# A fused sequence model block on one core: the injections of every second round of scan blocks 6 to 11 made beside attention, and the first experts' loads set apart

## The chip, the core and the metric

The kernel runs on one core of one Trainium2 chip. Five engines work side by side, each through its own list of instructions: PE (TensorE, matmuls), DVE (VectorE), ACT (ScalarE), POOL (GpSimd) and SP (SyncE), which here only issues DMAs. They are held together by semaphores: an instruction can wait until a counter has reached a number, and all that stands behind it in the list of its engine then waits too. The metric is device time in microseconds, from start to end of one execution; smaller is better. Between two versions of this kernel a difference of about 0.2%, or 2.6 us, can just be told from none.

## What is computed

Two layers over a sequence of 2048 tokens with 128 channels. The second layer carries nearly all of the time, and the change is in it alone: a selective scan in both directions, an attention with 16 heads whose sums go through a mixture of eight experts, and the sum of both.

```python
def step(h, ins):                       # 256 channels x 16 states, 2048 steps, forward and backward
    dt_t, u_t, B_t, C_t = ins
    h = exp(dt_t[..., None] * A) * h + (dt_t * u_t)[..., None] * B_t[:, None, :]
    y_t = einsum('bdn,bn->bd', h, C_t)
...
y = (y + u * Dp) * silu(z)
out_scan = einsum('bld,ed->ble', y, Wout)
...
o = softmax(q @ k.T / sqrt(D)) @ v      # 16 heads of 8 channels
x = x + (o @ wo + bo)
idx = argmax(layernorm(x) @ gate_w + gate_b)
moe = y_of_expert[idx]                  # relu(h @ w1[e] + b1[e]) @ w2[e] + b2[e]
return x + moe
```

(The inputs of the attention and of the scan are both normed from the same x; `out_scan` of both directions and the attention's result are added.)

## The kernel before

**Three stages** follow each other. `layer0_stage` computes the first layer. `front_stage` computes the attention and, ahead of it and beside it, the inputs of the scan, which go to DRAM: dt, dt times u (`dtu_d`), u, z, and the rows of B and C (`bc_d`). `tail_stage`, from about 878 us on, runs the scan, and beside it the experts.

**The scan** is cut into 8 chunks of 512 steps (4 forward, 4 backward), each chunk into 2 blocks of 128 channels: 16 blocks, numbered 0 to 15. A block is done in 4 rounds (q = 0 to 3, four of the 16 states each), a round in 4 tiles (j = 0 to 3, 32 channels each). A tile is 128 partitions x 512 steps. Rounds are numbered r = 0 to 63 and tiles k = 4r + j; block i has the rounds 4i to 4i + 3. Block 0 is done during attention; the loop of the tail runs over rounds 4 to 63. A tile takes four steps:

- ACT makes the decay exp(dt A) in one of four PSUM banks (line 1608), and later copies the last column of the state to `last` (line 1620);
- POOL makes the **injection** dtu times B, for two tiles (0 and 1, or 2 and 3) in one instruction of 128x1024 into `inject`, four tiles deep (line 1536);
- DVE runs the **scan** over decay and injection (line 1811), in place in PSUM, or into one of four buffers `hp` when POOL is to weigh the tile;
- the **weighing** with C goes to `hc`, which has two buffers, one for each parity of the round. `on_pool(k)` says which tiles are weighed by POOL (line 1521, 128x512 each); the others are DVE's (line 1737), tiles 1 and 2 as one instruction of 128x1024 where both are its own. In a round of blocks 5 to 12 POOL weighs tile 0, and tile 3 too where r % 3 is 1.

PE then adds the 4 tiles of a round into `y_bank` (line 1943, `sums(r)`), and in the first round of each block DVE multiplies the finished block before it with z after its tile 3 (line 1748, `gate`). A weighing in round r waits for `summed` of round r - 2, and a gate for the sums of all rounds of its block.

**Order on POOL.** The loop over tiles makes the injection of tiles j, j + 1 at an even tile, and then weighs the tile that lies three back, if it is POOL's: `weigh(k - NI + 1)` with NI = 4. An injection waits until the scan of the tile whose buffer it takes is done.

**Blocks made ahead.** POOL is nearly idle in attention. For the blocks in `AHEAD` (1 to 4 and 13 to 15) `products` (line 755) makes the injections of tiles 2 and 3 of all four rounds there, one block in each of the attention steps s = 2 to 8, four instructions of 128x1024. SP loads their inputs one step earlier (`load_for_products`) and stores the results to `ahead_d`. In the tail SP brings them back, one round of 512 KB at a time, into three buffers `ahead` (`load_ahead`, line 1412), and waits for that until the scans of the round that used the buffer are done. An ahead round has no injection of tiles 2 and 3 on POOL; in exchange POOL weighs tiles 0 and 3 there, and in odd rounds tile 2.

**Order on SP in the tail.** A loop over rounds: ahead loads, in every fourth round the dt and dtu of the next block (`load_steps`, line 410, eight DMAs), in some rounds the four arrays of an expert for slot s (`load_expert`, line 1432 and on, in round 19 + 4n + m for slot 3n + m), in round 20 the gathered rows for all 23 slots in four DMAs (`load_rows`, line 1424), and u and z of the next block (line 428). PE takes the first rows in `turn_rows(0)` of round 20 (line 1886), before `sums(21)`.

**Block 0's inputs.** In attention steps 10 to 14 SP loads B and C for block 0 and the first rounds (`load_bc`, line 436, one set a step). POOL makes its injections in steps 13 to 15 (`early_inject`, line 769, pairs 0 and 1, then 2 to 4, then 5 to 7; pair p needs the set p // 2). In each step they stand ahead of `split_max` (line 742), which attention needs.

## Time and profile before

| | us |
|---|---|
| median of 3 runs | 1314.99 |
| lowest and highest | 1313.97, 1315.51 |
| the profiled execution | 1312.72 |
| its span, first to last instruction | 1311.0 |

The span is 1.7 us shorter than the profiled execution's own time; this lies around it. A profile shows for each engine when it was busy, and for an idle stretch what ended it. In the tail two or more engines are busy more than nine tenths of the time, so the busy shares alone don't say what bounds it; the order of single instructions, and which of them waits for which, has to be read.

### The profile page before, as it was taken

The page shows a single profiled execution, that of the slowest core. Times are in us where ns is not written, and L with a number is a line of the kernel's source. Part 1 is how long each engine was busy: PE and PEld are TensorE (multiplying, and loading weights), DVE is VectorE, ACT ScalarE, POOL GpSimd, SP SyncE. Part 2 cuts the span into 40 slices and gives each one's busy share as a digit, 9 for nine tenths or more (in the row PEclk, how much of TensorE's full clock was granted, in tenths as well). Part 3 has the DMA queues.
Part 4 walks back from the last instruction along what each step waited for, and adds up shares of the span by engine and source line. Part 5 has one row for each costly group of instructions (what it writes and reads, how often), then busy time and mean ns, then how long its engine had stood idle before and what let it go on. Part 6 is the DMA issues. An engine that isn't in the chain of part 4 may idle for free. (4 is left out here: it accounts for less than half of the span.)

```text
span 1311.0 us, 18381 instructions
## 1 busy us (share of the span) xinstructions
PE 1034.7 (79%) x6017; PEld 337.0 (26%) x6017; DVE 1175.0 (90%) x1728; ACT 891.9 (68%) x1352; POOL 545.3 (42%) x395
## 2 busy tenths in 40 slices
PE   2789996888888888888888888884755987978764
PEld 1443331111111111111111111131411444444311
DVE  7892667999999999999999999848899899999997
ACT  6354558777777777777778787876545667777642
POOL 5020112502332023300000302226779899999896
PEclk9989996999999999999999999995656587888766
DMA  3034332314303464220000010016648966675452
GB/s 102 0 109 166 143 130 82 124 49 114 113 19 124 141 160 133 61 80 30 17 17 21 13 34 18 1 58 164 156 129 213 215 173 155 167 174 155 117 163 63
DMA packets 92385, 134.50 MB, mean 103 GB/s; under 512 B 15059, under 2 KB 45578, under 8 KB 92290
## 3 DMA queue, kind: packets, MB, share of 16 engines
q1 hardware_dynamic: 91266, 131.23, 36.0%
q0 software_dynamic: 1024, 2.10, 0.6%
q8 instruction: 48, 0.79, 0.3%
q14 instruction: 47, 0.39, 0.1%
HBM read 92.75 MB, written 40.24 MB: 101 GB/s over the span
## 5 line engine op out<-in xcount | busy, mean ns | idle before, releaser
L923 DVE TENSOR_REDUCE at_mpart<-psum 128x1 f32<-128x512 f32 x1024 | 637.8, 684 | 42.2 <-PE psum L1104 39.0
L895 ACT ACTIVATE at_probs<-psum 128x1024 f32<-128x1024 f32 x512 | 495.4, 1022 | 141.1 <-PE psum L1134 140.3
L1104 PE MATMUL psum<-at_ks,at_qs 56*128 56x512 bf16 x1024 | 202.3, 392 | 101.1 <-DVE at_mpart L923 100.4
L1147 PE MATMUL psum<-at_probs,at_vg 128*32 128x512 f32 x2048 | 273.6, 606 | 0.7 <-ACT at_probs L895 0.6
L1536 POOL TENSOR_TENSOR t_inject<-shared 128x1024 f32<-128x1024 f32 x92 | 215.6, 2355 | 29.4 <-POOLq L60 19.3
L742 POOL CAST at_m<-at_mneg 128x16 bf16<-128x16 f32 x16 | 4.0, 252 | 481.6 <-DVE at_mneg L928 476.0
L1608 ACT ACTIVATE psum<-shared,aneg 128x512 f32<-128x512 f32 x240 | 164.0, 691 | 48.7 <-DVE t_hc L1737 37.9
L1134 PE MATMUL psum<-at_qs,at_ks 59*128 59x512 bf16 x1024 | 156.6, 378 | 7.4 <-ACT at_probs L895 6.2
L1104 PEld LDWEIGHTS psum<-at_ks,at_qs 56*128 56x128 bf16 x1024 | 49.3, 93 | 423.5 <-DVE at_mpart L923 408.1
L1943 PE MATMUL psum<-t_hc,stack 128*32 128x512 f32 x480 | 95.5, 880 | 74.6 <-POOL t_hc L1521 48.5
L1521 POOL TENSOR_TENSOR t_hc<-t_hp,shared 128x512 f32<-128x512 f32 x100 | 126.0, 1271 | 32.6 <-DVE t_hp L1811 30.2
L1811 DVE TENSOR_TENSOR_SCAN psum<-psum,last,t_inject 128x512 f32<-128x512 f32 x88 | 109.0, 1274 | 5.6 <-ACT psum L1608 4.3
L1737 DVE TENSOR_TENSOR t_hc<-psum,shared 128x1024 f32<-128x1024 f32 (+1 forms) x90 | 86.8, 964 | 0.0
L1859 PE MATMUL psum<-t_bc_rows,t_sel 32*128 32x512 f32 x108 | 81.9, 896 | 0.0
L1620 ACT ACTIVATE last<-psum 128x1 f32<-128x1 f32 x99 | 16.5, 167 | 92.8 <-DVE t_hc L1737 92.4
L1811 DVE TENSOR_TENSOR_SCAN t_hp<-psum,last,t_inject 128x512 f32<-128x512 f32 x56 | 71.3, 1272 | 6.1 <-ACT psum L1608 3.5
L755 POOL TENSOR_TENSOR shared<-shared 128x1024 f32<-128x1024 f32 x28 | 65.2, 2360 | 0.0
L1134 PEld LDWEIGHTS psum<-at_qs,at_ks 59*128 59x128 bf16 x1024 | 50.1, 96 | 57.1 <-ACT at_probs L895 27.1
L728 POOL TENSOR_TENSOR shared<-shared 128x1024 f32<-128x1024 f32 x8 | 22.3, 2806 | 98.0 <-DVE shared L975 98.0
L1076 PE MATMUL psum<-mp_xm,mp_taps 128*128 128x512 f32 x128 | 61.6, 632 | 0.0
L1147 PEld LDWEIGHTS psum<-at_probs,at_vg 128*32 128x32 f32 x2048 | 40.3, 108 | 61.4 <-issue 59.5
L1943 PEld LDWEIGHTS psum<-t_hc,stack 128*32 128x32 f32 x480 | 12.8, 129 | 120.1 <-POOL t_hc L1521 69.8
(262 smaller groups left out, 1143.9 us busy)
## 6 DMA issues: line engine op xcount, KB each, us to landing
shared<-mp_dt_d SPq DMA_DIRECT2D x64, 256.0 KB, 5.8
mp_ahead_d<-shared SPq DMA_DIRECT2D x7, 2048.0 KB, 7.9
t_ahead<-mp_ahead_d SPq DMA_DIRECT2D x28, 512.0 KB
t_w<-in_w SPq DMA_DIRECT2D x46, 256.0 KB
shared<-mp_bc_d SPq DMA_DIRECT2D x152, 64.0 KB, 3.0
shared<-mp_dtu_d SPq DMA_DIRECT2D x36, 256.0 KB, 9.3
shared<-mp_dtu_d SPq DMA_DIRECT2D x56, 128.0 KB, 4.3
...
```

Of the source, the lines that this page charges most:

```text
L895: act.activation(probs[:, u_ % 2, p, :], s_pair[p], ACT.Exp, scale=float(HD) ** -0.5).then_inc(probs_ready, 1)
L923: dve.reduce_max(mpart[:, s % 2, 2 * jp + b, i, kc:kc + 1], ring[x % 3], AX.X).then_inc(ring_free, 1)
L1104: pe.matmul(ring[z_ % 3], qs[half(b, DQ), buf, of_pair(jp, c * CH + i * P, P)], ks[half(b, DQ), buf, of_pair(jp, kc * CH, CH)], start=True ...
L1134: mm = pe.matmul(s_banks[p][b], ks[half(b, DM), g % 2, of_pair(p, kt * P, P)], qs[half(b, DM), g % 2, of_pair(p, c * CH, CH)], start=True, ...
L1147: mm = pe.matmul(o_bank[VW * j:VW * (j + 1), :], vg[:, g % 2, kt, j, :], probs[:, u_ % 2, j // 2, CH * (j % 2):CH * (j % 2 + 1)], start=(k ...
L1521: pool.tensor_tensor(hc[:, r % 2, j, :], hp[:, by_pool[k] % NHP, :], cs[:, (NQ * (i // NB) + q) % NBC, :], ALU.mult).then_inc(pool_weighed, 1)
L1536: pool.tensor_tensor(inject[:, x % NI:x % NI + 2, :], dus[:, i % 2, j:j + 2, :], bs[:, m % NBC, :].unsqueeze(1).to_broadcast([P, 2, CH]), ...
L1608: act.activation(decay[k % ND], dts[:, i % 2, j, :], ACT.Exp, scale=S.aneg[:, n // NCH, m:m + 1])\
L1737: dve.tensor_tensor(hc[:, r % 2, j:j + n, :], decays[:, j:j + n, :], cs[:, m % NBC, :].unsqueeze(1).to_broadcast([P, n, CH]), ALU.mult).th ...
L1811: dve.tensor_tensor_scan(h, decay[k % ND], added, last[:, k % PC:k % PC + 1] if n % NCH else 0.0, ALU.mult, ALU.add).then_inc(scanned, 1)
L1859: pe.matmul(out, sel[:, NQ * o + q, :], bc_rows[:, n % 2, :], start=True, stop=True).then_inc(side_full, 1)
L1943: mm = pe.matmul(y_bank[GC * j:GC * (j + 1), :], S.stack[:, :], hc[:, r % 2, j, :], start=False, stop=(q == NQ - 1), tile_position=(0, GC ...
```

## The change

`AHEAD` becomes a list of groups of 8 pairs of tiles at most. The seven blocks of before stay. Three groups are new, of two blocks each (6 and 7, 8 and 9, 10 and 11): of these only rounds q = 1 and 3 are made ahead, so 12 rounds, all with an odd number. `AHEAD_AT` gives the place of a round in `ahead_d`. The products of the new groups are made in attention steps 9 to 11, and the loads of B and C for block 0 are moved from steps 10 to 14 into steps 12 to 14 (sets 0 and 1, then 2 and 3, then 4).

```diff
-AHEAD = 1, 2, 3, 4, 13, 14, 15
+AHEAD = [((i,), range(NQ)) for i in (1, 2, 3, 4, 13, 14, 15)] + [((2 * n, 2 * n + 1), (1, 3)) for n in (3, 4, 5)]
+AHEAD_AT = {(i, q): (g, m * len(qs) + x) for g, (blocks, qs) in enumerate(AHEAD)
+            for m, i in enumerate(blocks) for x, q in enumerate(qs)}
...
-                if s == 10:
+                if s == 12:
                     sp.wait_ge(a_st, 16 * len(AHEAD))
-                if 10 <= s < 10 + Inputs.NBC:
-                    first.load_bc(S, sp, s - 10, first_in[s - 4])
+                if 12 <= s < 15:
+                    for m in ((0, 1), (2, 3), (4,))[s - 12]:
+                        first.load_bc(S, sp, m, first_in[m + 6])
...
+            def products(g):
+                pool.wait_ge(a_in, 16 * SP4 * sum(len(blocks) + len(qs) for blocks, qs in AHEAD[:g + 1]))
+                if g:
+                    pool.wait_ge(a_st, 16 * g)
+                blocks, qs = AHEAD[g]
+                for m in range(len(blocks)):
+                    for x in range(len(qs)):
+                        pool.tensor_tensor(first.products[:, m * len(qs) + x, :, :], first.some_dus[:, m, :, :],
+                                           first.some_bs[:, x, :].unsqueeze(1).to_broadcast([P, 2, CH]), ALU.mult).then_inc(a_made, 1)
...
         def is_ahead(k):
 
-            return k // PB in AHEAD and k % NJ >= 2
+            return (k // PB, k // NJ % NQ) in AHEAD_AT and k % NJ >= 2
 
         def on_pool(k):
             r, j = divmod(k, NJ)
             if SCATTER <= r < SCATTER + MOVE or GATHER <= r < GATHER + MOVE:
-                return r // NQ in AHEAD and (j == 0 or j == 3 and r % 2 == 1)
-            if r // NQ in AHEAD:
+                return is_ahead(NJ * r + 2) and (j == 0 or j == 3 and r % 2 == 1)
+            if is_ahead(NJ * r + 2):
                 return j in (0, 3) or j == 2 and (r < SCATTER or r % 2 == 1)
-            return j == 0 or j == 3 and r % 3 == 1
+            return j == 0 or j == 3 and r % 3 == 1 and not is_ahead(NJ * r + 6)
...
-                if (s := slot_at(r, -2)) is not None:
+                if 0 <= r - FIRST_SLOT + 6 < W:
+                    load_expert(r - FIRST_SLOT + 6)
+                if (s := slot_at(r, -2)) is not None and s >= W:
                     load_expert(s)
...
-                if r == SCATTER + MOVE:
-                    for n in range(NX):
-                        load_rows(n)
+                if r >= SCATTER + MOVE and (r - SCATTER - MOVE) % 6 == 0 and (r - SCATTER - MOVE) // 6 < NX:
+                    load_rows((r - SCATTER - MOVE) // 6)
```

So in the odd rounds of blocks 6 to 11 POOL makes one injection in place of two and weighs tiles 0, 2 and 3; in their even rounds it makes two injections and weighs tile 0 alone. The experts of slots 0 to 3 are loaded in rounds 15 to 18 instead of 19, 20, 21 and 23, and the four parts of the gathered rows in rounds 20, 26, 32 and 38. The other edits size the buffers for a group of two blocks (in `Inputs`, `load_steps`, `load_for_products`) and look up the place of a round in `load_ahead`.

**POOL, rounds 24 to 27 (block 6).** `t_inject` is an injection of two tiles, `t_hc<-t_hp` a weighing. Before:

```order
L1536 TENSOR_TENSOR t_inject<-shared 128x1024 x2
L1521 TENSOR_TENSOR t_hc<-t_hp,shared 128x512
L1536 TENSOR_TENSOR t_inject<-shared 128x1024 x2
L1521 TENSOR_TENSOR t_hc<-t_hp,shared 128x512
L1536 TENSOR_TENSOR t_inject<-shared 128x1024 x2
L1521 TENSOR_TENSOR t_hc<-t_hp,shared 128x512 x2
```

And after, rounds 24 to 26 and the first injection of round 27:

```order
L1545 TENSOR_TENSOR t_inject<-shared 128x1024
L1545 TENSOR_TENSOR t_inject<-shared 128x1024
L1530 TENSOR_TENSOR t_hc<-t_hp,shared 128x512
L1545 TENSOR_TENSOR t_inject<-shared 128x1024
L1530 TENSOR_TENSOR t_hc<-t_hp,shared 128x512
L1545 TENSOR_TENSOR t_inject<-shared 128x1024
L1530 TENSOR_TENSOR t_hc<-t_hp,shared 128x512
L1545 TENSOR_TENSOR t_inject<-shared 128x1024
L1530 TENSOR_TENSOR t_hc<-t_hp,shared 128x512 x2
L1545 TENSOR_TENSOR t_inject<-shared 128x1024
```

In row 4 stands the one injection of round 25, and in row 5, right behind it, the weighing of tile 0 of that same round. Before, the injection of tiles 2 and 3 stood between the two.

**DVE, the end of round 27 to round 29 (blocks 6 and 7).** `psum` and `t_hp` are scans, by where they write; `t_gated` is the gate. After:

```order
L1820 SCALAR_TENSOR_TENSOR t_hp<-psum,last,t_ahead 128x512
L1820 SCALAR_TENSOR_TENSOR t_hp<-psum,last,t_inject 128x512
L1820 SCALAR_TENSOR_TENSOR psum<-psum,last,t_inject 128x512
L1677 TENSOR_TENSOR res<-res,psum 128x512
L1820 SCALAR_TENSOR_TENSOR psum<-psum,last,t_inject 128x512 x2
L1746 TENSOR_TENSOR t_hc<-psum,shared 128x1024
L1757 TENSOR_TENSOR t_gated<-shared,psum 128x512
L1820 SCALAR_TENSOR_TENSOR t_hp<-psum,last,t_inject 128x512
L1746 TENSOR_TENSOR t_hc<-psum,shared 128x512
L1820 SCALAR_TENSOR_TENSOR psum<-psum,last,t_inject 128x512
L1820 SCALAR_TENSOR_TENSOR t_hp<-psum,last,t_ahead 128x512
L1746 TENSOR_TENSOR t_hc<-psum,shared 128x512
```

Before, tile 0 of round 28 to the gate:

```order
L1811 SCALAR_TENSOR_TENSOR t_hp<-psum,last,t_inject 128x512
L1737 TENSOR_TENSOR t_hc<-psum,shared 128x512
L1811 SCALAR_TENSOR_TENSOR psum<-psum,last,t_inject 128x512
L1668 TENSOR_TENSOR res<-res,psum 128x512
L1811 SCALAR_TENSOR_TENSOR psum<-psum,last,t_inject 128x512
L1811 SCALAR_TENSOR_TENSOR t_hp<-psum,last,t_inject 128x512
L1737 TENSOR_TENSOR t_hc<-psum,shared 128x1024
L1748 TENSOR_TENSOR t_gated<-shared,psum 128x512
```

The even round keeps its weighings of 128x1024 and, behind tile 0 of the next round, of 128x512; the odd round has one of 128x512 left.

**SP, round 20.** Before, from `load_steps` on:

```order
L410 DMA shared<-mp_dt_d 32x4x512 x4
L410 DMA shared<-mp_dtu_d 32x4x512 x4
L1432 TENSOR_LOAD t_eid
L1432 ISA x2
L1433 ISA
L1433 DMA t_w1<-in_w1 128x512
L1434 ISA
L1434 DMA t_b1<-in_b1 128x4
L1435 DMA t_w2<-in_w2 128x4x128
L1437 ISA
L1437 DMA t_b2<-in_b2 1x128
L1424 DMA t_x<-t_rows 128x6x128 x3
```

After, down to the loads for the next block:

```order
L1420 DMA t_ahead<-mp_ahead_d 128x1024 x2
L412 DMA shared<-mp_dt_d 32x4x512 x4
L412 DMA shared<-mp_dtu_d 32x4x512 x4
L1432 DMA t_x<-t_rows 128x6x128
L433 DMA shared<-mp_u_d 128x512
L433 DMA shared<-mp_z_d 128x512
```

The expert has gone from ahead of the rows, and one part of the rows is loaded there instead of four.

## Rows read from the trace of the kernel before

**Rows 1.** The page: the span, and the busy time of each engine.

```profile
span 1311.0 us, 18381 instructions
PE 1034.7 (79%) x6017; PEld 337.0 (26%) x6017; DVE 1175.0 (90%) x1728; ACT 891.9 (68%) x1352; POOL 545.3 (42%) x395
```

**Rows 2.** Windows of the tail: length, busy us per engine, clock, DMA share.

```profile
1029.70:1043.00 13.30, 13.30 (x40) 7.29 (x39) 9.27 (x10) 8.91 (x23) 10.93 (x7) 0.50 0.86 197
1045.30:1202.10 156.80, 129.89 (x686) 70.26 (x685) 154.07 (x146) 109.43 (x294) 150.98 (x81) 0.83 0.71 167
```

**Rows 3.** DVE in order of time: start, duration, what; round 27 into 28.

```profile
1066.29 0.67 DVE L1737 TENSOR_TENSOR t_hc<-psum,shared 128x512 f32<-128x512 f32 x1
1066.87 1.28 DVE L1811 TENSOR_TENSOR_SCAN psum<-psum,last,t_inject 128x512 f32<-128x512 f32 x1
1068.06 0.67 DVE L1668 TENSOR_TENSOR res<-res,psum 128x512 f32<-128x512 f32 x1
...
1071.01 1.20 DVE L1737 TENSOR_TENSOR t_hc<-psum,shared 128x1024 f32<-128x1024 f32 x1
1072.13 0.68 DVE L1748 TENSOR_TENSOR t_gated<-shared,psum 128x512 f32<-128x512 f32 x1
1072.72 1.28 DVE L1811 TENSOR_TENSOR_SCAN t_hp<-psum,last,t_inject 128x512 f32<-128x512 f32 x1
```

**Rows 4.** POOL in order of time, around round 33.

```profile
1095.31 4.68 POOL L1536 TENSOR_TENSOR t_inject<-shared 128x1024 f32<-128x1024 f32 x2
1099.94 1.27 POOL L1521 TENSOR_TENSOR t_hc<-t_hp,shared 128x512 f32<-128x512 f32 x1
1101.18 4.67 POOL L1536 TENSOR_TENSOR t_inject<-shared 128x1024 f32<-128x1024 f32 x2
```

**Rows 5.** DVE: the scans of tile 0 in rounds 25 and 47.

```profile
1045.88 1.27 DVE L1811 TENSOR_TENSOR_SCAN t_hp<-psum,last,t_inject 128x512 f32<-128x512 f32 x1
...
1189.27 1.27 DVE L1811 TENSOR_TENSOR_SCAN t_hp<-psum,last,t_inject 128x512 f32<-128x512 f32 x1
```

**Rows 6.** POOL at round 52, the first ahead round behind block 12.

```profile
1218.89 2.35 POOL L1536 TENSOR_TENSOR t_inject<-shared 128x1024 f32<-128x1024 f32 x1
1223.26 1.27 POOL L1521 TENSOR_TENSOR t_hc<-t_hp,shared 128x512 f32<-128x512 f32 x1 [2.02 <-DVE t_hp L1811]
```

**Rows 7.** DVE: the scan of tile 0 in round 52.

```profile
1221.91 1.27 DVE L1811 TENSOR_TENSOR_SCAN t_hp<-psum,last,t_inject 128x512 f32<-128x512 f32 x1
```

**Rows 8.** The chain that ended last, in order of time, near 1018 us.

```profile
1018.00 7.66 DMA t_x<-t_rows
```

**Rows 9.** SP in order of time, round 20.

```profile
1008.67 4.46 SPq L410 DMA_DIRECT2D shared<-mp_dtu_d  x4
```

**Rows 10.** PE in order of time, rounds 20 to 23.

```profile
1025.80 0.45 PE L1886 MATMUL psum<-ident,t_x 128*128 128x128 f32 x1 [2.57 <-DMA t_x<-t_rows]
1026.17 1.93 PE L1943 MATMUL psum<-t_hc,stack 128*32 128x512 f32 x8
...
1033.96 1.94 PE L1943 MATMUL psum<-t_hc,stack 128*32 128x512 f32 x8
...
1043.89 1.21 PE L1943 MATMUL psum<-t_hc,stack 128*32 128x512 f32 x8
```

**Rows 11.** DVE in round 21 into 22.

```profile
1023.21 0.66 DVE L1737 TENSOR_TENSOR t_hc<-psum,shared 128x512 f32<-128x512 f32 x1
```

**Rows 12.** POOL in attention: two groups of products, an early injection, the next split_max.

```profile
500.09 9.31 POOL L755 TENSOR_TENSOR shared<-shared 128x1024 f32<-128x1024 f32 x4
541.41 9.31 POOL L755 TENSOR_TENSOR shared<-shared 128x1024 f32<-128x1024 f32 x4
...
752.32 2.35 POOL L769 TENSOR_TENSOR mp_w_in<-shared 128x1024 f32<-128x1024 f32 x1
787.88 0.20 POOL L742 CAST at_m<-at_mneg 128x16 bf16<-128x16 f32 x1 [33.21 <-DVE at_mneg L928]
```

**Rows 13.** SP in attention: loads of B and C in steps 11 to 13.

```profile
673.25 3.66 SPq L436 DMA_DIRECT2D shared<-mp_bc_d  x8
714.57 4.65 SPq L436 DMA_DIRECT2D shared<-mp_bc_d  x8
...
755.80 4.49 SPq L436 DMA_DIRECT2D shared<-mp_bc_d  x8
```

42 lines of the change are left out of this document (19 added, 23 removed).

## The prediction

> **What bounds the kernel now.** I read the page first [rows 1]: a span of 1311.0 us, DVE busy for 90% of it, POOL for 42%. The change moves work out of rounds 24 to 47 of the tail, so the window over these rounds comes next [rows 2]: 156.8 us long, DVE busy 154.07, POOL 150.98. Both are full there, and neither number says what a change on both brings. For that I read single instructions. On DVE a scan takes 1.19 us from start to start, a weighing of 128x512 0.58, one of 128x1024 1.12, and a gate or an addition to `res` 0.59 [rows 3]. On POOL two injections take 4.63, so 2.31 each, and a weighing 1.24 [rows 4].
>
> A pair of rounds, one even (E) and one odd (O), is the unit of the changed pattern. Before, DVE has in it 8 scans (9.52), two weighings of 1024 (2.24), on average 1.33 of 512 (0.77; 16 of the 24 rounds have one), half a gate and a quarter of an addition (0.44): 12.97 us. POOL has 4 injections (9.24) and 2.67 weighings (3.31): 12.55 us. The measured pair takes (1189.27 - 1045.88) / 11 = 13.04 us [rows 5]. So DVE bounds these rounds, with POOL half a microsecond behind it, and every other engine has room.
>
> **The change, rounds 24 to 47, by busy time.** POOL loses 12 injections (12 x 2.31 = 27.7) and gains 16 weighings (from 32 to 48: 16 x 1.24 = 19.8): 7.9 us less. DVE: in the 12 odd rounds the weighing of 1024 becomes one of 512 (12 x 0.54 = 6.5), 8 of them lose the one of tile 3 (8 x 0.58 = 4.6), and 4 even rounds get one back (2.3): 8.8 us less. Per pair DVE would need 12.97 - 0.73 = 12.24, POOL 3 x 2.31 + 4 x 1.24 = 11.89. If nothing else counted, the rounds would be 8.8 us faster.
>
> **The same, by order.** What counts is what each waits for. In the changed list of POOL the weighing of tile 0 of an odd round stands directly behind the injection that this tile needs. DVE can't scan O0 before the injection has ended, and POOL can't go on before the scan has: POOL stands for one whole scan in each pair. The trace has one such place, at round 52: injection at 1218.89, weighing of the same tile at 1223.26 with 2.02 us idle before it, released by DVE [rows 6]; the scan between them starts at 1221.91, and from its start to POOL's is 1.35 us [rows 7]. From one O0 to the next the loop is: weighing O0, injection E01, weighing O2, injection E23, weighings O3 and E0, injection O01, scan O0, which is 4 x 1.24 + 2 x 2.31 + 2.35 (the last injection, to its end) + 1.35 = 13.28 us. No buffer shortens it, since the list of POOL holds all of it. DVE fits in: with the end of scan O0 as 0, E2 can start at 7.2 (its injection ends then), E3 at 8.4, the weighing at 9.6, a gate at 10.7 to 11.3, and O0 comes at 12.0; DVE is idle about 1 us a pair. The pair thus takes 13.28 instead of 13.04. Eleven pairs cost 11 x 0.24 = 2.6 us; in the four that lie in rounds 32 to 39 a scan without a state from before is some 0.05 shorter, which I leave out. The start of round 24 and the end of round 47 I take as equal. Term: **+2.6 us** instead of -8.8.
>
> **PE at the gates.** POOL's weighing of O3 ends at 8.4 on this scale, 2.3 us ahead of the gate; on DVE it stood 4.7 us ahead of it (three scans and a weighing of 1024). And `sums` of the odd round stands behind PE's side work of the even one. At the lower clock (0.50, so 1.2 GHz) an even round with B and C to spread and all three expert steps keeps PE from 1033.96 to 1043.89, 9.9 us [rows 10]. It starts at 0.6, so `sums(O)` would start at 10.5 and end at 12.4, where the gate is due at 10.7; O0 then comes at 13.0, 1.0 us late. This can happen at the gates of rounds 32, 40 and 48, whose even rounds have the spreading. At the higher clock it can't. The window has a mean clock of 0.83 [rows 2], so I take one of three: **+1.0 us**, bounds 0 and 3.0.
>
> **Block 5, rounds 20 to 23.** The chain that ended last goes through the load of the rows, from 1018.00 for 7.66 us [rows 8]. PE sits idle for 2.57 us, from 1023.23, until they land, and does `sums(21)` at 1026.17 [rows 10]. Then it is busy without a gap at the lower clock to 1043.89, and DVE, which waits for ACT and by it for PE, is busy 9.27 of the 13.3 us from 1029.70 [rows 2]: 4.0 us idle. In the change SP issues the first part of the rows right behind `load_steps`, whose last DMA ends at 1008.67 + 4.46 = 1013.13 [rows 9], 4.9 us earlier; with the same 7.66 us it lands at 1020.8, before PE asks for it. `sums(21)` then waits for the weighing of tile 3 alone, which ends at 1023.87 [rows 11], and starts 2.3 us earlier. As PE is the bound up to 1043.89, DVE gets these back one for one: **-2.3 us**. The bounds are 0 (the rows land no earlier) and -4.0 (all the idle time of DVE).
>
> A rule bears on that lower bound. In the trace the clock is 0.50 while PE is busy without a gap from 1029.70 to 1043.00, and at 1043.89 the same sums take 1.21 us instead of 1.94 [rows 2, 10]. The Trainium skill, TensorE: Matmul & The Clock Gate, Part 1, says that the throttled clock is the resting state and that activity lifts it. By that rule a PE without the gap at 1023 would be fast sooner, and the term would be up to -4.0 in place of -2.3. The trace has no run without the gap, so the sum stays with -2.3.
>
> **What is hidden.** *Products in attention*: 12 more instructions on POOL, three times 9.31 us. Two steps with products start 541.41 - 500.09 = 41.32 apart [rows 12], two without 714.57 - 673.25 = 41.32 [rows 13]. Cost 0, bound 0.1 a step; the cover is POOL's idle time in a step of 41 us. *B and C of block 0 two steps later*: pair 4 of the early injections ran at 752.32, and its set is now issued from 755.80 on [rows 12, 13]. POOL waits there some 10 us, with `split_max` queued behind; but that one starts at 787.88 only after 33 us of idle time for DVE's maxima. Cost 0. *Experts 0 to 3 in rounds 15 to 18*: SP issues about 2 to 4 us more in each, ahead of loads that are due two rounds (13 us) later. Nothing waits for them in the trace of before; cost 0, with the bound of one late transfer as PE saw it, 2.6 us [rows 10]. *The 12 ahead loads*: 6.3 MB more in a window that moved 167 GB/s with DMA busy 0.71 [rows 2]; 24% more bytes make that 0.88. They are issued four rounds ahead. A gain could come only from the thinner traffic in rounds 19 to 23; it is in the -4.0.
>
> **Sum.** +2.6 + 1.0 - 2.3 = +1.3 us on the profiled execution's 1312.72 (span 1311.0 and 1.7 around it), so 1314.0. The median of the runs is 2.3 above that execution; on it the forecast is 1314.99 + 1.3 = **1316.3 us**.
>
> **Rivals.** *DVE stays the bound and its savings count.* It speaks for it that DVE is busier than POOL in the window and both lose 8 to 9 us; against it, the loop above, which the list of POOL fixes. If the loop took less than 12.24: -8.8 - 2.3 = -11.1, 1303.9 us. *PE decides.* If PE is at 1.2 GHz before all three gates, and the rows bring nothing because the rest of the traffic is as dense (0.86 in block 5 [rows 2]): +2.6 + 3.0 = +5.6, 1320.6 us. It decides from the point where `sums` of an odd round starts later than 9.5 us behind scan O0. This is the case that ends on the slower side. *The spacing of the loads does nothing*, the rest as forecast: +3.6, 1318.6. *The clock rises sooner in block 5 and no gate is late*: +2.6 - 4.0 = -1.4, 1313.6.
>
> **How the numbers follow.** A difference under 0.2% (2.6 us) can't be told from none. The forecast with its own range of 1313.6 to 1318.6 has a chance of 0.60; DVE's savings in whole or large part 0.16; PE at the gates, late transfers or both, above 1318.6, 0.19; something between 1306 and 1313 0.05. Faster than 1312.4 is then 0.19. Slower than 1317.6 is the 0.19 and a part of the forecast's own range (0.13): 0.32. The same: 0.49. The range from 1311 to 1322 leaves out the first rival and little else.
>
> **What would show it.** In the profile after: POOL idle some 1.3 us before the weighing that follows the single injection of each odd round, released by a scan into `t_hp`; tile 0 of rounds 25 and 47 some 146 us apart instead of 143.4; DVE idle about 12 us in these rounds, ended by POOL's injection; no wait of PE for `t_x` in round 20, and the sums of round 23 some 2.3 us earlier against round 20. The forecast is wrong if that distance comes out near 135 us (the loop is no loop), or over 149 (PE or DMA decides), or if attention's steps are longer than 41.3 us.

## The result, and the profile after

| | before | after |
|---|---|---|
| median (20 runs each) | 1315.26 us | 1318.03 us |
| lowest and highest | 1310.09, 1318.50 | 1315.55, 1321.86 |
| span of the profiled execution | 1311.0 us | 1315.6 us |

The ratio is 1.0022, with a 95% interval of 1.0015 to 1.0030: the changed kernel is slower by 2.9 us. The interval leaves out 1, but it reaches to both sides of the 0.2% that can just be told from none. The forecast was 1316.3, with a range of 1311 to 1322. By the prediction's own classes, 1318.03 lies just inside "slower than 1317.6", to which it had given 0.32, and not in "the same", with 0.49.

The page of the changed kernel, its span and its busy times, answers to [rows 1]:

```profile
span 1315.6 us, 18475 instructions
PE 1039.8 (79%) x6017; PEld 338.2 (26%) x6017; DVE 1167.0 (89%) x1724; ACT 892.9 (68%) x1352; POOL 566.9 (43%) x411
```

DVE has 8.0 us less to do than before and the span is 4.6 us longer, so the saved work became waiting. To see where, I cut the span at three gates, which DVE does at the end of rounds 20, 24 and 48 (start, duration, instruction):

```profile
1015.99 0.67 DVE L1757 TENSOR_TENSOR t_gated<-shared,psum 128x512 f32<-128x512 f32 x1
...
1043.88 0.68 DVE L1757 TENSOR_TENSOR t_gated<-shared,psum 128x512 f32<-128x512 f32 x1
...
1206.64 0.67 DVE L1757 TENSOR_TENSOR t_gated<-shared,psum 128x512 f32<-128x512 f32 x1
```

The same three gates stand at 1014.32, 1045.29 and 1202.12 in the kernel before. So:

| stretch | before | after | difference |
|---|---|---|---|
| start to gate of round 20 | 1014.3 | 1016.0 | +1.7 |
| block 5, to gate of round 24 | 31.0 | 27.9 | -3.1 |
| blocks 6 to 11, to gate of round 48 | 156.8 | 162.8 | +5.9 |
| to the end | 108.9 | 109.0 | +0.1 |

**Blocks 6 to 11.** The windows of the changed kernel over the end of block 5 and over these six blocks (length; busy us of PE, PEld, DVE, ACT and POOL; granted clock, DMA share, GB/s) answer to [rows 2]:

```profile
1029.45:1043.00 13.55, 13.55 (x52) 7.10 (x50) 12.27 (x12) 10.16 (x30) 12.79 (x7) 0.65 0.44 93
1043.88:1206.64 162.76, 134.10 (x686) 71.65 (x684) 146.75 (x142) 109.61 (x293) 142.54 (x84) 0.80 0.81 206
```

In the second row DVE is idle for 16.0 us and POOL for 20.2; before it was under 3 us and about 6 [rows 2]. By releaser the profile puts most of DVE's idle time down to ACT's decays (10.6 us) or to nothing that it shows (4.9). The times of the single scans say otherwise: 10.6 us of it lie before scans that start 0.1 us behind the end of a POOL injection, with the decay ready 1.2 us or more before. The forecast had about 12 us, ended by the injection. Another 3.2 us belong to one slow pair of rounds, described below. The reason stands in POOL's list, here around round 33 (start, duration, instruction, and in brackets the idle time before it and what ended it):

```profile
1095.41 2.35 POOL L1545 TENSOR_TENSOR t_inject<-shared 128x1024 f32<-128x1024 f32 x1
1099.19 1.27 POOL L1530 TENSOR_TENSOR t_hc<-t_hp,shared 128x512 f32<-128x512 f32 x1 [1.43 <-DVE t_hp L1820]
1100.43 2.37 POOL L1545 TENSOR_TENSOR t_inject<-shared 128x1024 f32<-128x1024 f32 x1
1102.76 1.26 POOL L1530 TENSOR_TENSOR t_hc<-t_hp,shared 128x512 f32<-128x512 f32 x1
1103.99 2.34 POOL L1545 TENSOR_TENSOR t_inject<-shared 128x1024 f32<-128x1024 f32 x1
1106.29 2.48 POOL L1530 TENSOR_TENSOR t_hc<-t_hp,shared 128x512 f32<-128x512 f32 x2
1108.74 2.35 POOL L1545 TENSOR_TENSOR t_inject<-shared 128x1024 f32<-128x1024 f32 x1
```

The order is the one of the prediction's loop. After the single injection of the odd round POOL stands still for 1.43 us until DVE has scanned tile 0; that is the one wait of POOL in the loop (1.39 to 1.45 us in ten of the twelve odd rounds), and from one such injection to the next it takes 1108.74 - 1095.41 = 13.33 us. Before, POOL went straight from the injections into the weighing [rows 4].

From tile 0 of round 25 (1044.47) to tile 0 of round 47 (1193.57) it is 149.10 us; before it was 143.39 [rows 5]. Ten of the eleven pairs take 13.28 to 13.40 us, 13.33 on average. One, from round 39 to round 41, takes 15.76. There DVE waits three times, for ACT, whose decays end right before these scans start:

```profile
1146.79 1.29 DVE L1820 TENSOR_TENSOR_SCAN psum<-psum,last,t_inject 128x512 f32<-128x512 f32 x1 [1.97 <-ACT psum L1617]
1148.50 1.29 DVE L1820 TENSOR_TENSOR_SCAN psum<-psum,last,t_inject 128x512 f32<-128x512 f32 x1 [0.41 <-ACT psum L1617]
1150.61 1.29 DVE L1820 TENSOR_TENSOR_SCAN psum<-psum,last,t_inject 128x512 f32<-128x512 f32 x1 [0.82 <-ACT psum L1617]
```

ACT in turn waits for PE's spread of B and C (first row), and PE is at its lower level: behind a wait of 3.36 us for POOL it becomes slower, and a spread takes 3.78 us instead of 1.98, or 1.2 in place of 2.4 GHz (the other two rows):

```profile
1145.58 0.60 ACT L1582 ACTIVATE shared<-psum 128x512 f32<-128x512 f32 x1 [1.87 <-PE psum L1868]
```

```profile
1134.18 1.57 PE L1952 MATMUL psum<-t_hc,stack 128*32 128x512 f32 x8 [3.36 <-POOL t_hc L1530]
...
1143.47 3.78 PE L1868 MATMUL psum<-t_bc_rows,t_sel 32*128 32x512 f32 x4
```

The drop as such isn't new. In the kernel before, PE drops at the same place, behind a wait of 1.61 us for POOL, but it is back at the higher level in the next spread:

```profile
1134.91 3.78 PE L1859 MATMUL psum<-t_bc_rows,t_sel 32*128 32x512 f32 x4
...
1142.70 2.21 PE L1859 MATMUL psum<-t_bc_rows,t_sel 32*128 32x512 f32 x4
```

The granted clock is 0.50 from 1133.0 to 1143.2 there, and from 1134.6 to 1151.7 in the changed kernel. So what differs is how long the lower level lasts.

**Block 5.** SP issues the first part of the rows at 1016.27 (second row; the first is the loads of dt times u before it), after 1.4 us of waiting for the scatter that writes them:

```profile
1010.36 4.49 SPq L412 DMA_DIRECT2D shared<-mp_dtu_d  x4
1016.27 0.38 SPq L1432 DMA_DIRECT2D t_x<-t_rows  x1
```

PE still waits for them, 1.79 us in place of 2.57 [rows 10], but the sums of round 22 now run in part, and the spread behind them wholly, at the higher level:

```profile
1026.68 0.45 PE L1895 MATMUL psum<-ident,t_x 128*128 128x128 f32 x1 [1.79 <-DMA t_x<-t_rows]
1027.06 1.94 PE L1952 MATMUL psum<-t_hc,stack 128*32 128x512 f32 x8
...
1034.85 1.42 PE L1952 MATMUL psum<-t_hc,stack 128*32 128x512 f32 x8
1036.20 1.98 PE L1868 MATMUL psum<-t_bc_rows,t_sel 32*128 32x512 f32 x4
```

Before, the clock was 0.50 until 1043 [rows 2]. Counted from the gate of round 20, it rises after 19.6 us here and after 29.9 us before.

**The 1.7 us before round 20** can't be laid on the change. From `split_max` of the attention step at about 499 us to the first injection of the tail it is 379.23 us before (499.07 to 878.30) and 379.24 after (499.72 to 878.96), and this stretch holds all the new products. Of the rest, 0.65 us arise ahead of it, where the change does nothing, and 1.1 between that first injection and the scan of tile 0 of round 4. This last stretch takes 6.2 us or 7.1 to 7.3, the one or the other in kernels of both kinds (7.1 in e2, which has the old program ahead of the tail, 6.2 in e6, which has the new one). From that scan to the gate of round 20 it is 129.8 us before and 129.7 after. Over all profiled kernels of this study the gate of round 20 stands between 1014.07 and 1016.95, with the program ahead of it changed or not (table below).

### The profile page after: what moved, and what is told of

Read it like the earlier page. It is cut to its first block and busy times, and to the rows that moved or that the text cites. A ratio compares the mean times of both kernels' runs of the same rounds, so it can differ in the third digit from the quotient of the medians.

```text
span 1315.6 us, 18475 instructions
## 1 busy us (share of the span) xinstructions
PE 1039.8 (79%) x6017; PEld 338.2 (26%) x6017; DVE 1167.0 (89%) x1724; ACT 892.9 (68%) x1352; POOL 566.9 (43%) x411
## 5 line engine op out<-in xcount | busy, mean ns | idle before, releaser
L1545 POOL TENSOR_TENSOR t_inject<-shared 128x1024 f32<-128x1024 f32 x80 | 187.9, 2351 | 21.0 <-POOLq L60 19.3
L1530 POOL TENSOR_TENSOR t_hc<-t_hp,shared 128x512 f32<-128x512 f32 x116 | 145.9, 1268 | 53.4 <-DVE t_hp L1820 52.3
L1820 DVE TENSOR_TENSOR_SCAN psum<-psum,last,t_inject 128x512 f32<-128x512 f32 x78 | 97.8, 1277 | 7.2 <-ACT psum L1617 6.0
L763 POOL TENSOR_TENSOR shared<-shared 128x1024 f32<-128x1024 f32 x40 | 93.1, 2358 | 0.0
L1746 DVE TENSOR_TENSOR t_hc<-psum,shared 128x512 f32<-128x512 f32 (+1 forms) x86 | 77.8, 904 | 0.0
L1820 DVE TENSOR_TENSOR_SCAN t_hp<-psum,last,t_inject 128x512 f32<-128x512 f32 x50 | 63.7, 1274 | 11.0 <-ACT psum L1617 6.1
L734 POOL TENSOR_TENSOR shared<-shared 128x1024 f32<-128x1024 f32 x8 | 22.3, 2801 | 98.8 <-DVE shared L983 98.8
L1820 DVE TENSOR_TENSOR_SCAN t_hp<-psum,last,t_ahead 128x512 f32<-128x512 f32 x38 | 48.2, 1268 | 3.1 <-ACT psum L1617 3.1
```

The costliest lines, as they stand in the source:

```text
L763: pool.tensor_tensor(first.products[:, m * len(qs) + x, :, :], first.some_dus[:, m, :, :], first.some_bs[:, x, :].unsqueeze(1).to_broadcas ...
L1530: pool.tensor_tensor(hc[:, r % 2, j, :], hp[:, by_pool[k] % NHP, :], cs[:, (NQ * (i // NB) + q) % NBC, :], ALU.mult).then_inc(pool_weighed, 1)
L1545: pool.tensor_tensor(inject[:, x % NI:x % NI + 2, :], dus[:, i % 2, j:j + 2, :], bs[:, m % NBC, :].unsqueeze(1).to_broadcast([P, 2, CH]), ...
L1820: dve.tensor_tensor_scan(h, decay[k % ND], added, last[:, k % PC:k % PC + 1] if n % NCH else 0.0, ALU.mult, ALU.add).then_inc(scanned, 1)
```

## The experiments

Times are the medians, ratios those to the kernel before on the same chip, with the 95% interval. The last three columns are from one profile each: the gate of round 20, block 5, and blocks 6 to 11, all by the gates as above.

| kernel | time us | ratio | gate 20 | block 5 | blocks 6-11 |
|---|---|---|---|---|---|
| before | 1315.26 | 1 | 1014.3 | 31.0 | 156.8 |
| after | 1318.03 | 1.0022 (1.0015 to 1.0030) | 1016.0 | 27.9 | 162.8 |
| e2_loads_only | 1311.53 | 0.9975 (0.9963 to 0.9987) | 1014.4 | 27.7 | 157.7 |
| e3_ahead_only | 1320.80 | 1.0045 (1.0028 to 1.0061) | 1015.8 | 30.9 | 163.2 |
| e4_products_only | 1312.62 | 0.9983 (0.9969 to 0.9997) | 1014.4 | 30.9 | 160.5 |
| e1_weigh_later | 1311.58 | 0.9975 (0.9959 to 0.9990) | 1016.9 | 27.9 | 156.0 |
| e6_fill | 1316.79 | 1.0024 (1.0011 to 1.0037) | 1014.1 | 28.1 | 163.0 |
| e5_tile2_dve | 1309.38 | 0.9967 (0.9953 to 0.9982) | 1014.2 | 28.1 | 154.1 |
| e8_all_late | 1302.04 | 0.9901 (0.9887 to 0.9916) | 1016.2 | 27.9 | 149.3 |
| e9_pe_filled | 1318.42 | 1.0019 (1.0006 to 1.0032) | 1017.0 | 30.5 | 159.9 |
| e10_late_filled | 1304.40 | 0.9929 (0.9911 to 0.9947) | 1016.0 | 28.0 | 149.4 |
| e_rows_only | 1315.20 | 1.0007 (0.9995 to 1.0019) | 1016.9 | 31.0 | 156.8 |
| e_exp_only | 1313.11 | 0.9991 (0.9972 to 1.0011) | 1014.2 | 28.0 | 156.7 |
| e11_rows_first | 1300.68 | 0.9889 (0.9869 to 0.9910) | 1014.1 | 27.0 | 150.3 |

### The change in its parts

**The loads alone** (`e2_loads_only`): the kernel before, with the two edits of SP's loop, of the experts and of the rows.

```diff
-                if (s := slot_at(r, -2)) is not None:
+                if 0 <= r - FIRST_SLOT + 6 < W:
+                    load_expert(r - FIRST_SLOT + 6)
+                if (s := slot_at(r, -2)) is not None and s >= W:
                     load_expert(s)
...
-                if r == SCATTER + MOVE:
-                    for n in range(NX):
-                        load_rows(n)
+                if r >= SCATTER + MOVE and (r - SCATTER - MOVE) % 6 == 0 and (r - SCATTER - MOVE) // 6 < NX:
+                    load_rows((r - SCATTER - MOVE) // 6)
```

> The kernel before with only the loads set apart: experts 0 to 3 in rounds 15 to 18, the rows in rounds 20, 26, 32 and 38. Theory A has -3.1 us for it from the profile after (gate of round 8 to gate of round 24: 122.7 us before, 119.6 after), so a ratio of 0.9970 to 0.9985 with the stretch from round 25 to 47 at 143.4 as before. The rival, that the faster block 5 comes from something else in the change or is chance of the clock, gives 0.9995 to 1.0005.

**The injections made ahead alone** (`e3_ahead_only`): the changed kernel, with these two edits taken back.

> The changed kernel with the loads of experts and rows as before: only the injections made ahead are left of the change. Theory A: the loop's 13.3 us a pair in rounds 25 to 47 (146 to 149 us for the stretch) and block 5 as slow as before, so 3 to 6 us slower than before, ratio 1.002 to 1.005. If the parts depend on each other, so that the SP queue is late without the earlier expert loads, the stretch would be longer than 150 us and the ratio above 1.006.

**The products alone** (`e4_products_only`): like e3, and the tail doesn't use the new groups.

```diff
-            return (k // PB, k // NJ % NQ) in AHEAD_AT and k % NJ >= 2
+            return k // PB in (1, 2, 3, 4, 13, 14, 15) and k % NJ >= 2
```

> The changed kernel's front stage (three more groups of products in attention, stored, and B and C of block 0 loaded later), with the tail of the kernel before, which doesn't use the twelve new rounds. Theory A holds that this is hidden: ratio 0.9995 to 1.0008. The rival is the 1 to 1.7 us by which the tail of the changed kernel stands later up to round 8 in its profile: then 1.001 to 1.0015.

The loads alone give 0.25% (3.3 us), the injections made ahead cost 0.45% (5.9 us), and the two together make 2.6 us, close to the 2.9 of the whole change. The profiles put both where they belong: e2 has the short block 5 (27.7) and nearly the old blocks 6 to 11, e3 the old block 5 (30.9) and the long blocks 6 to 11 (163.2). The products alone cost nothing. Their ratio is even below 1 (0.9983), which no stretch of their profile explains: that profile is of the slowest of the twelve executions (1316.35 us). And it has a surprise of its own, to which I return below: blocks 6 to 11 take 160.5 us in it, with the very program of before in the tail.

### POOL's loop

**Tile 0 weighed later** (`e1_weigh_later`). If POOL's wait behind the single injection closes the loop, it has to go once the next injection is put ahead of the weighing. This edit of the changed kernel does so for tile 0 of the odd rounds of blocks 6 to 11:

```diff
+            def late(k):
+                r, j = divmod(k, NJ)
+                return j == 0 and r > R0 and is_ahead(k + 2) and not is_ahead(k - 2) and not is_ahead(k + 6)
...
-                weigh(k - NI + 1)
+                if late(k - NI):
+                    weigh(k - NI)
+                if not late(k - NI + 1):
+                    weigh(k - NI + 1)
```

> The changed kernel with one difference: on POOL the weighing of tile 0 of an odd round of blocks 6 to 11 stands one instruction later, behind the first injection of the next round. The same instructions, the same bytes, the same DMAs. Theory A (the loop: weighing O0, three injections, three weighings, scan O0, 13.3 us a pair) says that POOL no longer stands for the scan, so DVE with 12.24 us a pair bounds these rounds: tile 0 of round 25 to tile 0 of round 47 falls from 149.1 us in the changed kernel to 135 to 138, and the time to some 10 us below the kernel before (ratio 0.991 to 0.994). Rival B (the ahead loads, PE's clock or the later weighings of tile 3 are what costs) says that the order of one weighing does nothing: 147 to 150 us for the stretch and a ratio of 1.001 to 1.003.

The ratio went from 1.0022 to 0.9975, a gain of 6.2 us, less than expected. From tile 0 of round 25 to that of round 47 it takes 143.48 us, not 135 to 138. POOL's list of this kernel shows why:

```profile
1073.12 1.28 POOL L1530 TENSOR_TENSOR t_hc<-t_hp,shared 128x512 f32<-128x512 f32 x1
1075.48 1.28 POOL L1530 TENSOR_TENSOR t_hc<-t_hp,shared 128x512 f32<-128x512 f32 x1 [1.08 <-DVE t_hp L1827]
1076.70 2.36 POOL L1549 TENSOR_TENSOR t_inject<-shared 128x1024 f32<-128x1024 f32 x1
1079.01 2.51 POOL L1530 TENSOR_TENSOR t_hc<-t_hp,shared 128x512 f32<-128x512 f32 x2
1081.47 4.67 POOL L1549 TENSOR_TENSOR t_inject<-shared 128x1024 f32<-128x1024 f32 x2
```

The first row is the weighing of tile 0, now without a wait. But the second, that of tile 2, waits 1.08 us for its scan, and behind it stand E23, O3, E0 and O01. I had removed one ring and not looked for the next: scan O0 (1071.17), O1, O2, weighing O2, E23, O3, E0, injection O01, scan O0 (1083.92), 12.75 us. Eleven of these are 140.3 us. The rest is mostly one slow pair again, at another place: from round 31 to round 33 it takes 15.57 us, and PE's clock is at the lower level from 1080.9 to 1098.0.

**Tiles 0 and 2 weighed later** (`e8_all_late`): the same with `j in (0, 2)`.

```diff
-                return j == 0 and r > R0 and is_ahead(k + 2) and not is_ahead(k - 2) and not is_ahead(k + 6)
+                return j in (0, 2) and r > R0 and is_ahead(NJ * r + 2) and not is_ahead(NJ * r - 2) and not is_ahead(NJ * r + 6)
```

> The changed kernel, in which POOL weighs tiles 0 and 2 of an odd round of blocks 6 to 11 one injection later than it did: order of a pair of rounds: injection O01, E01, weighing O0, injection E23, weighings O2, O3, E0. In the run before this one, in which only the weighing of tile 0 was moved, a pair still took 12.75 us (13.33 in the changed kernel), and POOL again waited, now 0.7 to 1.1 us ahead of the weighing of tile 2. Theory (POOL's order waits for DVE, and that wait sets the pair): with tile 2 moved too the ring is gone, a pair takes what DVE computes in it, 11.8 us without and 12.4 us with a gate, so about 12.2; from tile 0 of round 25 to that of round 47 133 to 138 us (143.5 with tile 0 alone moved, 149.1 in the changed kernel), the time 1303 to 1307, ratio 0.991 to 0.994. Rival 1 (TensorE at its lower clock sets the pair through ACT's decays): the pair stays at 12.6 to 13, time 1309 to 1313. Rival 2 (POOL's busy time sets it): POOL is busy 12.0 us a pair, as before the move, and what DVE gains is taken back: 1309 to 1312.

The theory holds, with a little more than it had promised in the time: 1302.04 us, ratio 0.9901, and 134.22 us from tile 0 of round 25 to that of round 47 (1044.67 to 1178.89), 12.20 a pair. Its window over blocks 6 to 11, and two of POOL's pairs:

```profile
1044.08:1193.38 149.30, 125.17 (x683) 69.73 (x682) 145.22 (x143) 109.06 (x295) 143.07 (x85) 0.84 0.90 227
```

```profile
1078.54 4.65 POOL L1549 TENSOR_TENSOR t_inject<-shared 128x1024 f32<-128x1024 f32 x2
1083.15 1.26 POOL L1530 TENSOR_TENSOR t_hc<-t_hp,shared 128x512 f32<-128x512 f32 x1
1084.38 2.35 POOL L1549 TENSOR_TENSOR t_inject<-shared 128x1024 f32<-128x1024 f32 x1
1086.69 3.71 POOL L1530 TENSOR_TENSOR t_hc<-t_hp,shared 128x512 f32<-128x512 f32 x3
```

POOL has nothing to wait for in them, and DVE is busy 145.22 of 149.30 us. With the same work as in the changed kernel these blocks are 13.5 us shorter; nothing else than the place of two weighings in POOL's list is different.

**The gap filled** (`e6_fill`). The counter-check: if the wait and not the work sets the pair, more work for POOL inside the wait must cost nothing. Here POOL weighs tile 3 of every even round too.

```diff
-            return j == 0 or j == 3 and r % 3 == 1 and not is_ahead(NJ * r + 6)
+            return j == 0 or j == 3 and (r % 3 == 1 or is_ahead(NJ * r + 6))
```

> The changed kernel, in which POOL weighs tile 3 of every even round of blocks 6 to 11 as well, 1.27 us more of work for POOL in each pair of rounds and 0.6 us less for DVE. In POOL's list it comes between the injection of tiles 0 and 1 of the odd round and the weighing of tile 0, so where POOL now waits 1.27 to 1.45 us. Theory (the wait sets the pair, not the work): a pair stays at 13.3 to 13.4 us, from tile 0 of round 25 to that of round 47 148 to 151 us, time 1316 to 1320, ratio 1.001 to 1.004. Rival (POOL's busy time sets the pair): a pair takes 1.2 us more, 162 us from round 25 to 47, time 1329 to 1333, ratio 1.011 to 1.014.

Met: ratio 1.0024 beside 1.0022, blocks 6 to 11 in 163.0 beside 162.8 us. POOL is busy 13.9 us more in them than in the changed kernel (156.42 beside 142.54), and its wait is down to 0.2 us. DVE is busy 6.5 us less (140.28 beside 146.75), and that brings nothing either:

```profile
1042.20:1205.23 163.03, 132.52 (x680) 70.98 (x680) 140.28 (x130) 108.69 (x291) 156.42 (x96) 0.79 0.82 206
```

```profile
1067.07 2.37 POOL L1545 TENSOR_TENSOR t_inject<-shared 128x1024 f32<-128x1024 f32 x1
1069.39 1.27 POOL L1530 TENSOR_TENSOR t_hc<-t_hp,shared 128x512 f32<-128x512 f32 x1
1070.88 1.27 POOL L1530 TENSOR_TENSOR t_hc<-t_hp,shared 128x512 f32<-128x512 f32 x1 [0.22 <-DVE t_hp L1820]
```

Such a POOL, busy for 96% of a window, looks like the bound; it was busy for 88% of it at the same length.

**One weighing less in the ring** (`e5_tile2_dve`): the changed kernel, with tile 2 of the odd rounds weighed by DVE.

```diff
-                return j in (0, 3) or j == 2 and (r < SCATTER or r % 2 == 1)
+                return j in (0, 3) or j == 2 and (r < SCATTER or r % 2 == 1) and not 24 <= r < 48
```

> The changed kernel, in which DVE and not POOL weighs tile 2 of the odd rounds 25 to 47: POOL has 1.27 us less in each pair of rounds, DVE 0.54 us more (tiles 1 and 2 as one instruction of 1.21 us in place of 0.67). Theory (the ring scan of tile 0, weighing of tile 0, E01, O2, E23, O3, E0, O01 sets the pair): with one weighing less in it the pair goes from 13.33 to 12.1 for POOL's ring, so that DVE's own 12.4 to 13.0 sets it: 12.75 on average, 140 to 143 us from tile 0 of round 25 to that of round 47, time 1309 to 1313, ratio 0.996 to 0.9985. Rival (DVE's work, or TensorE, sets the pair): the pair takes 13.3 or more, time 1318 to 1324.

Met: 1309.38 us, 139.99 us from round 25 to round 47, 12.73 a pair. DVE got more work and the kernel became 7 us faster (0.9967 beside 1.0022); DVE is busy 151.69 of 154.12 us there. This also beats the kernel before, although no weighing was moved in POOL's list.

### PE's clock in blocks 6 to 11

**PE kept busy in the waits** (`e9_pe_filled`). In the changed kernel PE waits for POOL's weighings 21.3 us in all between 1045 and 1200 us (how often, and the longest), before it 5.0:

```profile
PE psum L1952 <- POOL t_hc L1530: 21.3, 8, 3.6
```

```profile
PE psum L1943 <- POOL t_hc L1521: 5.0, 3, 2.4
```

The first row is of the changed kernel, the second of the kernel before. To see whether these waits bring the clock down, and whether that makes the slow pair, PE multiplies by zeros ahead of them:

```diff
+                if 24 <= r < 48 and r % 4 == 1:
+                    for m in range(2):
+                        for j in range(NJ):
+                            pe.matmul(y_bank[GC * j:GC * (j + 1), :], zeros[:, 0:GC],
+                                      S.xn1[:, 0:TPC, :].rearrange("p i d -> p (i d)"),
+                                      start=False, stop=False, tile_position=(0, GC * j))
                 pe.wait_ge(pool_weighed, by_pool[NJ * (r + 1)])
```

(One more line lets PE wait once, in the tail's side work, until the zeros are there.)

> The changed kernel, in which TensorE multiplies by zeros (two sets of four matmuls of 128x512, added to the sums, so that nothing changes) before it waits for POOL's weighing in rounds 25, 29, 33, 37, 41 and 45. There it now waits 3.1 to 3.6 us, and right after most of these waits its clock is at the lower level: the next sums take 1.94 us in place of 1.06, the spread of B and C 3.78 in place of 1.98, and behind one of them DVE waits 3.2 us in all for ACT, which waits for the spread. The fill takes 2.1 us at the higher clock and fits into the wait. Theory (the waits bring the clock down, and the lower clock costs the one slow pair of rounds): the waits shrink to 1.2 to 1.5 us, the granted clock from round 25 to 47 rises from 0.79 to 0.88 or more, the slow pair (15.76 us beside 13.3) goes, time 1314 to 1317, ratio 0.9985 to 1.001. Rival 1 (the clock falls at these places whatever TensorE does just before): the fill takes 3.9 us there and holds up the sums, the slow pair stays or there are more of them, time 1318 to 1322. Rival 2 (the slow pair has another cause): the clock rises, the time stays at 1317 to 1319.

Inside blocks 6 to 11 the theory holds. At round 29 the fill takes 1.92 us, the wait behind it 1.54 in place of 3.34, and the sums 1.07 in place of 1.94:

```profile
1081.20 1.92 PE L1953 MATMUL psum<-xn,t_zeros 128*32 128x512 f32 x16
1084.66 1.07 PE L1959 MATMUL psum<-t_hc,stack 128*32 128x512 f32 x8 [1.54 <-POOL t_hc L1530]
```

```profile
1047.49:1207.34 159.85, 134.16 (x781) 71.59 (x782) 146.53 (x142) 109.82 (x294) 141.91 (x84) 0.89 0.81 206
```

The granted clock of the window is 0.89 (0.80 in the changed kernel), the slow pair is gone, all pairs take 13.30 to 13.61 us, and rounds 25 to 47 147.16 in place of 149.10. The pair itself stays where POOL's loop puts it: the clock has no part in that. But the time isn't lower, 1318.42, and the expected 1314 to 1317 were missed. In the profiled execution 2.9 us are won here and 2.6 lost in block 5, which took 30.5 us: PE's clock stayed at the lower level there, with the loads of the changed kernel. One profile can't say whether the other eleven executions lost it in the same way, so why the median isn't lower stays open.

**The same on the kernel of e8** (`e10_late_filled`), with one set of four matmuls in place of two.

> The kernel with the weighings of tiles 0 and 2 both moved one injection later (1302.0 us), in which TensorE also multiplies by zeros (one set of four matmuls of 128x512) before the wait for POOL in rounds 25, 29, 33, 37, 41 and 45; the waits there are 1.5 to 2.0 us. That kernel has one slow pair of rounds behind round 45's wait (15.1 us in place of 12.3) in which DVE waits 2.2 us for ACT and POOL while TensorE runs at its lower clock. Theory (the wait brings the clock down): the slow pair goes, time 1299 to 1301, ratio 0.988 to 0.9895. Rival (clock falls anyway, by what comes before): time 1302 to 1304, ratio 0.990 to 0.992.

The waits shrank from 1.5 to 2.0 us to 0.5 to 1.0, but the slow pair behind round 47 stayed (14.96 us, in e8 15.09), and the time is not better (0.9929 beside 0.9901). These waits are not what brings the clock down there. What does, I haven't tried.

So the slow pair is only half settled. It comes by PE's lower level and ACT's wait; in the one profile of e9, with filled waits, it is gone. But it isn't the change's alone: e4, with the tail of before, has a slow pair in the same place, at round 40, 1.9 us longer than in the kernel before, and DVE waits there for ACT and POOL by 0.85, 0.41 and 0.82 us. The wait of PE for POOL ahead of it is 1.61 us, as in the kernel before; only the lower level lasts longer, from 1133.3 to 1150.4. It shows in the three profiles with the changed order in POOL's list (after, e3, e6) and in one of five with the old one (before, e2, e4, e_rows, e_exp), and that one is the slowest of its kernel's executions, while the other three lie within 0.8 us of their medians. This speaks for a share of the change in it. But e1 has its slow pair at round 32, and e8, e10 and e11 have theirs behind round 47, each under a long stretch at the lower level. One profile a kernel doesn't settle how much of its 2.4 us the change causes.

### Block 5

**The rows alone and the experts alone** (`e_rows_only`, `e_exp_only`): the kernel before, with one half each of e2's diff.

> The kernel before, in which only the four parts of the gathered rows are loaded in rounds 20, 26, 32 and 38; the experts are loaded as before. With both moved, block 5 (gate of round 20 to gate of round 24) went from 31.0 to 27.7 us and the kernel to 0.9975. Theory of the prediction (the rows land later than PE wants them, and splitting them brings the first ones sooner): block 5 shrinks by 2 to 3 us here, time 1311 to 1313, ratio 0.9975 to 0.999. Rival (the first experts' loads stand ahead of the rows on SP's queue, or PE's clock rises sooner once the experts are there): no gain here, block 5 stays at 30.5 to 31.5, ratio 0.9995 to 1.0005.

> The kernel before, in which only the experts of slots 0 to 3 are loaded in rounds 15 to 18; the rows are loaded all together in round 20. Theory of the prediction (the rows' split is what counts): block 5 shrinks by less than 1 us, ratio 0.999 to 1.0005. Rival (the experts' loads delay the rows): block 5 shrinks by 2 to 3 us here, ratio 0.9975 to 0.999.

The profiles are plain: with the rows alone block 5 takes 31.0 us, with the experts alone 28.0, so the experts' loads count and the splitting of the rows doesn't. The times lie on the same side (1.0007 and 0.9991), but the interval of the second takes in 1. The chain that ended last shows what the first part of the rows took from issue to landing; the first row is of e_rows_only, the second of e_exp_only:

```profile
1020.67 7.65 DMA t_x<-t_rows
```

```profile
1013.42 11.43 DMA t_x<-t_rows
```

PE waits for the first part alone, since each part has its own semaphore; so the 7.66 us of the kernel before [rows 8] are those of the first part too, and three more parts behind it made no difference there. Without the experts' loads in front it was issued 4.5 us sooner against the gate of round 20 and then took 3.8 us more. They land 11.4 us behind the gate of round 20 in e_rows_only, 10.7 in e_exp_only.

**The rows first** (`e11_rows_first`): the kernel of e8, in which the first part of the rows is issued ahead of the eight loads of dt and dtu.

```diff
+                if r == SCATTER + MOVE:
+                    load_rows(0)
                 if rest == 0 and 2 <= i + 1 < NN * NB:
                     load_steps(i + 1)
...
-                if r >= SCATTER + MOVE and (r - SCATTER - MOVE) % 6 == 0 and (r - SCATTER - MOVE) // 6 < NX:
+                if r > SCATTER + MOVE and (r - SCATTER - MOVE) % 6 == 0 and (r - SCATTER - MOVE) // 6 < NX:
                     load_rows((r - SCATTER - MOVE) // 6)
```

> The kernel with the weighings of tiles 0 and 2 both moved one injection later (1302.0 us), in which SP issues the first part of the gathered rows ahead of the eight loads of dt and dtu of the next block in round 20, and not behind them. In the runs so far the rows took 7.65 us from issue to landing where the experts' loads stood between them and dt and dtu, and 10.3 to 11.4 where they stood right behind dt and dtu, so that they landed 10.6 us behind the gate of round 20 in place of 11.3. Theory (the rows queue behind the 1.5 MB of dt and dtu): issued first, they take under 5 us, land 3 to 5 us sooner, TensorE waits for them not at all or under 0.3 us, sums(21) starts 1.5 to 1.9 us sooner against the gate of round 20, and block 5 (27.9 us there) takes 25.5 to 27; time 1299.5 to 1301.5, ratio 0.988 to 0.990. Rival 1 (the scatter of the rows ends only at about 2 us behind the gate, and a gathered load takes 7 us by itself): TensorE still waits over 1 us, block 5 stays at 27.5 to 28.5, time 1301 to 1303. Rival 2 (dt and dtu come too late, since SP waits for the scatter): a wait of ACT or POOL for them at round 24, time 1304 or more.

```profile
1009.93 0.37 SPq L1432 DMA_DIRECT2D t_x<-t_rows  x1
1010.34 1.97 SPq L412 DMA_DIRECT2D shared<-mp_dt_d  x4
```

```profile
1022.92 0.47 PE L1904 MATMUL psum<-ident,t_x 128*128 128x128 f32 x1
1023.78 1.93 PE L1961 MATMUL psum<-t_hc,stack 128*32 128x512 f32 x8 [0.39 <-DVE t_hc L1755]
...
1033.44 2.12 PE L1877 MATMUL psum<-t_bc_rows,t_sel 32*128 32x512 f32 x4
```

Issued first, the rows land 4.2 us after their issue, 0.1 us behind the gate of round 20 in place of 10.6. (The eight loads that stood in front are 256 KB each, so 2 MB in all, where the expectation has 1.5.) PE no longer waits for them, `sums(21)` starts 9.7 us behind that gate (11.1 in e8, 11.85 before) and block 5 takes 27.0 us. The scatter that SP waits for ends sooner too: SP issues the rows at 1009.93, where e8 with dt and dtu in front could do so at 1016.02 (against the gate of round 20, 4.1 us ahead of it and 0.1 ahead of it). So most of the rows' latency, 10.7 us in e8, was the loads in front of them. The time of 1300.68 us is 1.4 below e8's, and the intervals overlap; in the profiles block 5 is 0.9 us shorter than in e8, and blocks 6 to 11 are 1.0 longer. The gain stands in block 5 alone and isn't shown for the whole. With both moves in it, this kernel is 1.1% under the one before.

## Why the prediction was right, and where its steps failed

**The loop** was right. A pair of 13.28 us was worked out and ten pairs took 13.33; POOL's wait ahead of the weighing was put at some 1.3 us and is 1.39 to 1.45; and that DVE's saved work brings nothing against it is shown by e6 (more work, same time), e5 (less in the ring, faster) and e8 (no ring, 12.20 a pair, where the count of DVE's work had said 12.24). Of the 5.7 us that rounds 25 to 47 became longer, eleven pairs at this pace carry 11 x 0.29 = 3.2; the forecast was 2.6.

**PE at the gates** had the right engine, and with round 40 one of the three rounds it named, but the wrong path. No gate waits for PE. Its lower level reached DVE through the spread, ACT's copy and the decays, and cost 15.76 - 13.33 = 2.4 us on top of the loop, in place of 1.0, within the bounds of 0 to 3.0. With it the distance from round 25 to round 47 is 149.10 us, just over the 149 at which the prediction had called itself wrong ("PE or DMA decides"), and 3 us over the 146 that it had expected. The loop alone makes 146.6; the sign came true by the slow pair. I had looked at what PE does last, and the path to DVE goes through what it does first. How much of it is due to the change stays open.

**Block 5** had nearly the right size and a wrong mechanism. The step that failed is "with the same 7.66 us it lands at 1020.8": the latency was taken as a property of the load, while it was the time to clear the loads in front. The rows landed 10.6 us behind the gate of round 20, not 6.5, and the forecast sign, no wait of PE for `t_x`, didn't come. What gave 3.1 us instead of 2.3 is mostly PE's clock, which rose some 10 us sooner against the gate of round 20. e9 separates the two: its `sums(21)` starts 0.6 us sooner than before, its clock rises as late as before, and its block 5 is only 0.4 us shorter; the changed kernel's is another 2.6 shorter. The clock rose sooner in nine of ten profiled kernels with the experts loaded early, and in none of the four others; e9 is the one exception. What decides it isn't shown. In eight of the nine the rows land 10.4 to 10.7 us behind the gate of round 20 (in e11 0.1), and in e9 and the four others 10.8 to 11.4; but the last of the one group, e6 with 10.74, and the first of the other, e9 with 10.77, are too near each other to call this the cause. The bound of -4.0 was that of a closed gap, and e11, which closes it, is 4.0 us shorter than the kernel before. The prediction had used the Trainium skill, TensorE: Matmul & The Clock Gate, Part 1, which says that activity lifts the clock. That closing the gap makes it rise sooner isn't borne out: in e11, where PE doesn't wait for the rows, it rises 19.7 us behind the gate of round 20, and in the changed kernel, with 1.79 us of wait, after 19.6. The same part says that the place where the clock rises differs from run to run of one kernel. That agrees with e9 beside the changed kernel, which have the same loads there and a block 5 of 30.5 and 27.9 us, though these are two kernels with one profile each. I had weighed only the first of the two statements.

**What was hidden** stayed hidden. Products and the later loads of B and C cost nothing (379.23 and 379.24 us around them), although POOL waited longer for B and C than I had said, 14.95 us and not 10; 20.4 us were still left ahead of `split_max`. The ahead loads brought the DMA share to 0.81, not 0.88, and no wait for them shows.

```profile
722.05 4.80 POOL L777 TENSOR_TENSOR at_vg<-shared 128x1024 f32<-128x1024 f32 x2 [14.95 <-DMA shared<-mp_bc_d]
```

**The sum.** On the span +1.3 was forecast and +4.6 came: +1.7 ahead of round 20, which isn't the change's, +5.9 where 3.6 had been put, -3.1 where it was -2.3, and 0.1 at the end. On the medians it is +2.8; that the first term averages out there is likely, but not shown. That the result lies so near the forecast owes something to two errors of opposite sign: 2.3 us too little in blocks 6 to 11 and 0.8 too little gain in block 5.
